# Part of a norm and a weight split moved from the start of the query, key and value projection into the last group of the feed-forward part before it

## The reference, cut to what matters

```python
def _layernorm(x, axis=-1, eps=1e-05):
    m = jnp.mean(x, axis=axis, keepdims=True)
    v = jnp.var(x, axis=axis, keepdims=True)
    return (x - m) / jnp.sqrt(v + eps)

x = x + 0.5 * ffn(_layernorm(x))         # gate and up 512 -> 4096, gelu(gate) * up, down 4096 -> 512
x = x + attention(_layernorm(x))         # 16 heads of 32, causal, 2048 tokens, one batch
x = x + 0.5 * ffn(_layernorm(x))         # the same weights as the first
```

## Time and profile before

| | us |
|---|---|
| median of 3 runs (lowest, highest) | 3058.48 (3055.43, 3061.62) |
| the profiled execution, its own time | 3058.05 |
| its span in the trace | 3056.3 |
| PE busy | 2944.6 (96%) |
| DVE, ACT, POOL busy | 1878.1, 1060.1, 758.6 |
| ffn1: its last down matmul begins at | 1107.10 |
| items 0 to 15: first begins, work behind them begins | 1135.97, 1186.70 |

### The profile page before, as it was taken

How to read it: one execution, slowest core, us unless ns; L and a number is a source line. 1 busy time by engine, 2 the same in 40 slices (tenths; PEclk the granted TensorE clock), 3 DMA queues, 4 the chain that set the end, 5 groups by cost and what they waited for, 6 DMA issues and landing times. The chain is left out here.

```text
span 3056.3 us, 38836 instructions
## 1 busy us (share of the span) xinstructions
PE 2944.6 (96%) x13152; PEld 2208.8 (72%) x13152; DVE 1878.1 (61%) x3314; ACT 1060.1 (35%) x1797; POOL 758.6 (25%) x481
## 2 busy tenths in 40 slices
PE   5999999999999989999999999689999999999999
PEld 3788888888888858754454555368888888888887
DVE  7666565566565555566666665876556656556654
ACT  4322222222222222265565665243222222222222
POOL 4322222222222234400000002343222222222221
PEclk8999999999999989999999999799999999999999
DMA  3000000000000016822322331101000000000001
GB/s 96 21 28 22 27 27 21 21 27 24 24 27 21 1 45 130 220 54 52 62 55 52 62 78 64 45 14 33 23 21 27 21 27 27 21 21 27 21 14 55
DMA packets 120234, 126.75 MB, mean 41 GB/s; under 512 B 72728, under 2 KB 72984, under 8 KB 116820
## 3 DMA queue, kind: packets, MB, share of 16 engines
q1 hardware_dynamic: 120148, 125.71, 15.8%
HBM read 96.34 MB, written 29.34 MB: 41 GB/s over the span
## 5 line engine op out<-in xcount | busy, mean ns | idle before, releaser
L61 PE MATMUL psum<-ffn_x_high,ffn_w_high 128*128 128x512 f32 x2048 | 803.3, 392 | 18.6 <-DVE ffn_gelu L389 18.6
L62 PE MATMUL psum<-ffn_x_low,ffn_w_high 128*128 128x512 f32 x2048 | 799.2, 390 | 0.0
L63 PE MATMUL psum<-ffn_x_high,ffn_w_low 128*128 128x512 f32 x2048 | 798.9, 390 | 0.0
L526 POOL TENSOR_TENSOR ffn_inner<-ffn_gelu,ffn_inner 128x512 fp32r<-128x512 f32 x256 | 345.9, 1351 | 1156.8 <-ACT ffn_inner L471 1156.8
L379 DVE SCALAR_TENSOR_TENSOR ffn_gelu<-ffn_gelu,psum 128x512 f32<-128x512 f32 x256 | 175.9, 687 | 600.0 <-ACT ffn_gelu L464 599.9
L61 PEld LDWEIGHTS psum<-ffn_x_high,ffn_w_high 128*128 128x128 f32 x2048 | 386.1, 189 | 103.9 <-DVE ffn_gelu L389 21.9
L62 PEld LDWEIGHTS psum<-ffn_x_low,ffn_w_high 128*128 128x128 f32 x2048 | 385.9, 188 | 81.9 <-issue 2.0
L63 PEld LDWEIGHTS psum<-ffn_x_high,ffn_w_low 128*128 128x128 f32 x2048 | 385.8, 188 | 80.7
L61 PE MATMUL psum<-ffn_inner,ffn_w_high 128*128 128x512 f32 x1024 | 398.6, 389 | 0.2
L62 PE MATMUL psum<-ffn_inner,ffn_w_high 128*128 128x512 f32 x1024 | 398.4, 389 | 0.0
L63 PE MATMUL psum<-ffn_inner,ffn_w_low 128*128 128x512 f32 x1024 | 398.4, 389 | 0.0
(11 more groups left out here) (116 smaller groups left out, 3191.1 us busy)
## 6 DMA issues: line engine op xcount, KB each, us to landing
ffn_words<-packed SPq DMA_DIRECT2D x96, 256.0 KB
ffn_word_scales<-scales SPq DMA_DIRECT2D x96, 256.0 KB
qk_parts<-parts SPq DMA_DIRECT2D x32, 512.0 KB, 4.3
queries<-qk_parts SPq DMA_DIRECT2D x48, 256.0 KB, 4.1
keys<-qk_parts SPq DMA_DIRECT2D x48, 256.0 KB, 6.1
x<-x_in SPq DMA_DIRECT2D x4, 1024.0 KB, 14.5
v_parts<-parts SPq DMA_DIRECT2D x16, 256.0 KB, 4.7
values<-v_parts SPq DMA_DIRECT2D x16, 256.0 KB, 8.0
```

What stands on the lines that cost most here:

```text
L61: pe.matmul(out, w_high, x_high, start=first, stop=False, skip_group_check=True)
L62: pe.matmul(out, w_high, x_low, start=False, stop=False, skip_group_check=True)
L63: return pe.matmul(out, w_low, x_high, start=False, stop=last, skip_group_check=True)
L526: pool.tensor_tensor(inner[:, tb % 2, m, 1, :], product[m], f32(inner[:, tb % 2, m, 0, :]), ALU.subtract)\
```

## The change

- In ffn1's last group, POOL does `sum_pairs` of tb 0 for the projection's norm between its two tiles of tb 3, once all gate and up products are done and x of tb 0 is final. PE does `mean` 0 before `down(3)`, into bank 0. DVE does `centre` 0 between `add_down` of tb 2 and of tb 3.
- SP issues the load of `wv` when all gate and up products are done. Behind their last tile ACT makes `wv_high` and squares block 0, and POOL makes `wv_low`. All these buffers lie over ffn1's `x_high` and `x_low`, which are read no more then.
- `project_in` begins with `sum_square_pairs` 0 and `variance` 0. The constants (matrix of 1/512, eps, and the buffer `std`) exist once for the program, and are set once.
- In `project_in` PE's list becomes: variance 0, mean 1, mean 2, items 0 and 1, variance 1, items 2 and 3, mean 3, items 4 and 5, variance 2, items 6 to 9, variance 3, items 10 to 15. DVE's and ACT's lists are rearranged with it; `scale` is cut in two, `invert` (the reciprocal) and `scale` (the multiplications), so that an addition of a value item can stand between them.

```diff
@@ class Norm
-        act.activation(self.std[:], self.var_bank[tb % 2], ACT.Sqrt, bias=self.eps[:]).then_inc(self.std_ready, 1)
-
-    def scale(self, dve, tb):
+        act.activation(self.std[:], self.var_bank[tb], ACT.Sqrt, bias=self.eps[:]).then_inc(self.std_ready, 1)
+
+    def invert(self, dve, tb):
         dve.wait_ge(self.std_ready, tb + 1)
         dve.reciprocal(self.std[:], self.std[:]).then_inc(self.rstd_ready, 1)
+
+    def scale(self, dve, tb):
         dve.wait_ge(self.rstd_ready, tb + 1)
@@ class QkvAhead (new)
+        self.norm = Norm(nc, ctx, "qkv", x, None, None, [centred[:, i, :, :] for i in range(2)], squares, pairs[:],
+                         constants.std, constants.averager, constants.eps,
+                         [bank[0], bank[4], bank[5], bank[4]], 2 * bank[6:8], None)
...
+    def high(self, act):
+        act.wait_ge(self.wv_loaded, 16)
+        act.activation(self.wv_high[:], self.wv[:], ACT.Copy).then_inc(self.wv_high_ready, 1)
+
+    def low(self, pool):
+        pool.wait_ge(self.wv_high_ready, 1)
+        pool.tensor_tensor(self.wv_low[:], self.wv[:], f32(self.wv_high[:]), ALU.subtract)\
+            .then_inc(self.wv_low_ready, 1)
@@ ffn, SP
+            if ahead is not None:
+                sp.wait_ge(gate_up_ready, 2 * NTB * NGROUP)
+                sp.dma_start(ahead.wv[:], ahead.w_v).then_inc(ahead.wv_loaded, 16)
@@ ffn, PE, group
+                    elif ahead is not None:
+                        pe.wait_ge(product_ready, 2 * NTB * NGROUP - 1)
+                        ahead.norm.mean(pe, 0)
                     down(gg, s, tb)
@@ ffn, DVE, group
+                    if tb == NTB - 1 and last_group and ahead is not None:
+                        ahead.norm.centre(dve, 0)
                     add_down(gg, s, tb)
@@ ffn, ACT, behind the last group
+            if ahead is not None:
+                ahead.high(act)
+                ahead.norm.square(act, 0)
@@ ffn, POOL, group
+                    if tb == NTB - 2 and last_group and ahead is not None:
+                        gelu_tiles(gg, s, tb + 1, [0])
+                        pool.wait_ge(gate_up_ready, 2 * NTB * NGROUP)
+                        pool.wait_ge(down_free, KT * NTB * (NGROUP - 1) + 2 * KT)
+                        ahead.norm.sum_pairs(pool, 0)
+                        gelu_tiles(gg, s, tb + 1, [1])
...
+            if ahead is not None:
+                ahead.low(pool)
@@ project_in, PE
-            n.mean(pe, 0)
+            n.variance(pe, 0)
             n.mean(pe, 1)
-            n.variance(pe, 0)
             n.mean(pe, 2)
+            pe.wait_ge(ahead.wv_low_ready, 1)
+            value_items(range(0, 2))
             n.variance(pe, 1)
-            pe.wait_ge(wv_low_ready, 1)
-            value_items(range(0, 2))
+            value_items(range(2, 4))
             n.mean(pe, 3)
-            value_items(range(2, 4))
+            value_items(range(4, 6))
             n.variance(pe, 2)
-            value_items(range(4, 8))
+            value_items(range(6, 10))
             n.variance(pe, 3)
-            value_items(range(8, TT))
+            value_items(range(10, TT))
```

More of the change, by code:

```diff
@@ L114, in mean @@
         for k in range(2):
-            last = pe.matmul(self.mean_bank[tb % 2], self.averager[:], self.pairs[:, k, :],
+            last = pe.matmul(self.mean_bank[tb], self.averager[:], self.pairs[:, k, :],
                              start=(k == 0), stop=(k == 1))
@@ L144, in variance @@
         for k in range(2):
-            last = pe.matmul(self.var_bank[tb % 2], self.averager[:], self.squares[:, k, :],
+            last = pe.matmul(self.var_bank[tb], self.averager[:], self.squares[:, k, :],
                              start=(k == 0), stop=(k == 1))
@@ L222, in ffn @@
         n = Norm(nc, ctx, tag, x, x_high, x_low, [centred0[:, :, :], centred1[:, :, :]],
-                 squares[:, :, :], pairs[:, :, :], std, averager, eps,
-                 down_bank[0:2], down_bank[2:4], x_loaded)
+                 squares[:, :, :], pairs[:, :, :], constants.std, constants.averager, constants.eps,
+                 2 * down_bank[0:2], 2 * down_bank[2:4], x_loaded)
         words_loaded = [sem(f"words_loaded{p}") for p in range(NPIECE)]
@@ L314, in group @@
                         gate_up(gg + s, 1 - s, 0)
+                    elif ahead is not None:
+                        pe.wait_ge(product_ready, 2 * NTB * NGROUP - 1)
+                        ahead.norm.mean(pe, 0)
                     down(gg, s, tb)
+            if x_in is not None:
+                pe.wait_ge(constants.ready, 2)
             n.mean(pe, 0)
@@ L407, in group @@
                         unpack(gg + s, 1 - s, tb)
+                    if tb == NTB - 1 and last_group and ahead is not None:
+                        ahead.norm.centre(dve, 0)
                     add_down(gg, s, tb)
-            dve.memset(averager[:], 1.0 / D).then_inc(n.constants_ready, 1)
-            dve.memset(eps[:], EPS).then_inc(n.constants_ready, 1)
+            if x_in is not None:
+                dve.memset(constants.averager[:], 1.0 / D).then_inc(constants.ready, 1)
+                dve.memset(constants.eps[:], EPS).then_inc(constants.ready, 1)
             n.sum_pairs(dve, 0)
@@ L480, in group @@
                         weight_high(gg + s, 1 - s, tb)
-            act.wait_ge(n.constants_ready, 2)
+            if x_in is not None:
+                act.wait_ge(constants.ready, 2)
             weight_high(0, 0, GATE)
@@ L521, in weight_low, with gelu_tiles @@
                                    f32(w_high[s][:, :, piece, :]), ALU.subtract).then_inc(w_low_ready, 1)
-            def gelu_tiles(gg, s, tb):
-                for m in range(2):
+            def gelu_tiles(gg, s, tb, tiles=range(2)):
+                for m in tiles:
                     pool.wait_ge(inner_high_ready, 16 * gg + (8 * s + 2 * tb + m + 1))
@@ L800, in head_items_after, with project_in @@
     return ITEMS_BEFORE[len(ITEMS_BEFORE) * i // (steps + LEFT_TO_LAST):end]
-def project_in(nc, x, bank, w_v, b_v, w_qk, b_qk, qk_parts, v_parts, heads):
+def project_in(nc, x, bank, ahead, b_v, w_qk, b_qk, qk_parts, v_parts, heads):
     with ExitStack() as ctx:
@@ L828, in project_in @@
         parts = sb("parts", [P, ITEM_BANKS, 2, TB], F32R)
-        n = Norm(nc, ctx, "qkv", x, x_high, x_low, [heads.norm_centred[:, tb, :, :] for tb in range(2)],
-                 squares, heads.norm_pairs[:], std, averager, eps, bank[4:6], bank[6:8], None)
-        wv_loaded = sem("wv_loaded")
+        n = ahead.norm
+        n.x_high, n.x_low = x_high, x_low
         bias_loaded = sem("bias_loaded")
         wt_loaded = sem("wt_loaded")
-        wv_high_ready = sem("wv_high_ready")
-        wv_low_ready = sem("wv_low_ready")
         wt_high_ready = sem("wt_high_ready")
@@ L1533, in build @@
         bank = [psum[:, i, :] for i in range(8)]
-        ffn(nc, "ffn1", x, bank, packed, scales, x_in, None)
-        attend(nc, x, bank, w_v, b_v, w_qk, b_qk, w_out, b_out, qk_parts, v_parts, o_heads, sums, inverses)
-        ffn(nc, "ffn2", x, bank, packed, scales, None, out)
+        constants = NormConstants(nc, ctx)
+        ahead = QkvAhead(nc, ctx, x, bank, constants, w_v)
+        ffn(nc, "ffn1", x, bank, constants, packed, scales, x_in, None, ahead)
+        attend(nc, x, bank, ahead, b_v, w_qk, b_qk, w_out, b_out, qk_parts, v_parts, o_heads, sums, inverses)
+        ffn(nc, "ffn2", x, bank, constants, packed, scales, None, out, None)
 def laid_out(L0_attn_x, L0_attn_w_qkv, L0_attn_b_qkv, L0_attn_w_out, L0_attn_b_out,
```

95 lines of the change are left out of this document (51 added, 44 removed).

## The result

The changed kernel takes 3063.14 us (median of 20 runs, 3061.28 to 3066.13), the kernel before, run beside it, 3057.85 us (20 runs, 3053.5 to 3061.62). The ratio is 1.0018, its 95% interval 1.0012 to 1.0025: +5.3 us. The interval leaves out 1, so the change is a little slower, but by less than the 0.2% that the prediction took as the least that can be told from no change. The profiled execution's own time is 3062.0, its span 3060.2.

What follows compares the result with a forecast made beforehand. PE, bound before by the norm's latency and then its own work, becomes a chain of three latencies: 9.9 us won and given back, +0.6, plus 3.6 of clock, is +4.2 on 3058.05, so 3062.3 us; range 3057 to 3069.

Steps and rivals of the forecast that it cites:

- In the first FFN: End of the first FFN: mean 0 moves `down(3)` back by 1.45 us; `centre` 0 and the pairs cost nothing more.
- Cover of wv: First FFN: the load of wv (4.9 us) and its split (4.51 on POOL) finish in time, priced at nothing.
- The sum of squares (1.23): Start of the projection: DVE's sum for block 0 starts at 1110.05 and takes 1.23 us, so the variance begins at 1111.3.
- Block 0's latency: Projection, variance 0 to last low tile: 13.3 to 15.2 us, low 0 ending at 1125.6, 9.9 earlier than before.
- The latencies of blocks 1 to 3: Projection, each variance to its last low tile: 15.0, 14.4 and 13.3 us for blocks 1, 2 and 3.
- It must stand still: PE at items 4, 8 and 12: stalls waiting for low tiles, 5.1 us for block 2 and 4.0 for block 3.
- I take 1.2 per stall: PE's slow clock in the three stalls: 1.2 us each, 3.6 together, between nothing and about 3.1 per stall.
- the first rival: Every stall is followed by a slow stretch costing 3.1 us instead of 1.2: +10.8, 3068.9 us; chance 0.25.
- The reading of the slow rows: Trace before the change: slow stretches lie behind gaps of 2.6 and 7.8 us, with no row for shorter ones in series.
- 3.4 between each two: PE between two latencies: the last quarter of an item and one whole item, 0.68 + 2.72 = 3.4 us.
- 8.84 at the end: Behind block 3's last low tile: the last quarter of item 12 and items 13 to 15, 0.68 + 8.16, to 1187.3.
- The second rival: Projection: the stalls are hidden and PE stays the bound, about -10 us, 3048; chance 0.06.

Runs made afterwards that it cites:

- pool_wait: The changed kernel with POOL's sum of pairs of block 1 waiting until DVE's sum of squares of block 0 is done; 3059.87 us, ratio 1.0008.
- order_only: The kernel before with only the new order of items, variances and additions, nothing moved into the first FFN; 3069.95 us, ratio 1.0035.
- order_back: The changed kernel with PE's item order of before and DVE's additions moved to fit, the moved part kept; 3055.68 us, ratio 0.9992.
- warm: The changed kernel with two unused fp32 matmuls on PE ahead of items 8 and 12; 3062.58 us, ratio 1.0015.
- item_pad2: The changed kernel with 1760 unused bytes per partition ahead of the projection's own buffers; 3061.93 us, one run.
- combined: The changed kernel with the old item order, POOL's pairs behind DVE's squares, and DVE's sums of squares 2 and 3 earlier; 3048.84 us, ratio 0.9973.

## Why the prediction came out, step by step

The forecast was +4.2 (3062.3); measured is +5.3 by the medians (3063.14). Its mechanism stood; some of its terms did not, and errors of both signs met. Down the chain, predicted and measured:

| step | predicted | measured |
|---|---|---|
| last addition, next block | 1109.67, 1110.05 | 1109.30, 1109.63 |
| variance 0 begins | 1111.3 | 1113.09 |
| low 0 ends | 1125.6 (1124.6 to 1126.5) | 1127.97 |
| low 1 ends | 1144.0 | 1146.20 |
| low 2 ends | 1161.8 | 1164.03 |
| low 3 ends | 1178.5 | 1182.74 |
| work behind the items | 1187.3, with the clock 1190.9 | 1192.01 |

- **In the first FFN: right.** `down(3)` moved back by about 1.3 (the last matmul begins 1108.18 here, 6.98 behind mean 0) against 1.45, and the cover held: mean 0 waited for no pairs (0.23 behind the last down matmul), `centre` 0 took 2.29 and was done at 1105.41, the barrier took 0.33.
- **Cover of wv: right.** The load landed in time for ACT to split from 1100.92 to 1102.83, ahead of its squares at 1105.44, and POOL's `wv_low` ran from 1102.91 to 1107.54, before the barrier.
- **"The sum of squares (1.23)": wrong, by 2.17.** I took the duration from a row in which POOL read nothing beside it, although the same sum took 2.31 us where it ran among POOL's low tiles (at 1160.08 before), a slowdown that the prediction itself counts as 1.0 for block 2. POOL's sum of pairs 1 is released by the same barrier. pool_wait shows the price, alone and with its follow-up on variance 0: 3.1.
- **Block 0's latency: right in size** (14.88, within 13.3 to 15.2), though low 0 came outside its bounds, since the start above was late.
- **The latencies of blocks 1 to 3: right.** 15.0, 14.4 and 13.3 predicted, 14.58, 14.17 and 13.22 measured; the addition of item 2 held block 1's multiplications up by 0.4 (to 1138.07, the reciprocal being done at 1137.61), not 0.7.
- **"It must stand still": right.** From the end of the work ahead to the start of the last quarter, less the 2.1 us that three quarters take, the stalls are 3.5 at item 4, 5.0 at item 8 and 3.9 at item 12, predicted 4 (with mean 3 ahead of it), 5.1 and 4.0. order_only shows them without the head, order_back takes them away.
- **"I take 1.2 per stall", the clock: wrong in size and kind.** Behind items 4 and 12 the next steps ran at full clock (3.66 from low 1 to variance 2, as from low 0 to variance 1); only item 8 was followed by a stretch at 0.50, and took 5.49, 1.8 more than its likes. That is 1.8 instead of 3.6, and never 3.1 three times as the first rival had it. Why item 8 and not its likes isn't settled: the pad of 1760 bytes moved the slow stretch to item 12, the fill of warm to item 9, and order_only has one behind item 4 and one behind item 12. What the rows show is that PE did work in quarters in all three stalls, and that one of three was followed by 1.2 GHz, two of three in order_only. The passage of the Trainium skill on a PE that waits between short bursts, named with the first rival, is about waits in one piece; here the quarters cut each stall into waits of at most 1.7 us. As the first rival applied it, it asked for a slow stretch behind all three, and the trace doesn't agree, beyond that one.
- **The reading of the slow rows: incomplete.** The prediction says that the slow stretches of before lie behind gaps of 2.6 and 7.8, and that the trace has no row for shorter ones in series. It has: mean 1 waited 2.49, and variance 0 behind it only 0.83, took 3.78 and ran at half the clock. That series stood for a dearer stall than the 1.2 taken.

```profile
1115.98 2.60 PE L115 MATMUL psum<-qkv_pairs,qkv_averager 128*128 128x512 f32 x4 [2.49 <-POOL qkv_pairs L104]
```

```profile
1118.00:1120.00 2.00, 1.17 (x2) 0.50 (x2) 1.86 (x2) 1.98 (x3) 1.33 (x1) 0.50 0.98 361
```

- **"3.4 between each two", and 8.84 at the end: too short, by 1.2 in all.** At full clock the link from a last low tile to the next variance took 3.66, and the end 9.27. An item at 2.80 instead of 2.72 is the smaller part, some 0.4: in item_pad2, with items at 2.72, a link still took 3.60. The other 0.8 is PE's restart behind a low tile: the last quarter's first matmul begins 0.05 behind the tile, and the next one 0.35 later (1128.02 and 1128.37) instead of 0.23. The prediction put that at nothing.

The sum: 2.2 for the sum of squares, 1.2 for the links and the end, and 0.6 for block 0's latency more than predicted, against 1.8 less on the clock, 0.7 on the latencies of blocks 1 to 3 and 0.4 in the FFN, gives the 1.1 between 1190.9 and 1192.01. That the total is near is in part luck.

The second rival (stalls hidden, -10) needed "low tiles within 9.3 us". combined got its -9 another way: by leaving four items behind variances 2 and 3, together with the two repairs on DVE and POOL. I had the cause in front of me (before, items 4 to 7 hid block 2's 14.4 us) and didn't ask whether the head with the old order would keep both.

## What to carry to other kernels

When work is moved ahead, what it wins is kept only if enough independent work still stands behind each link of the chain: here a variance with four items behind it (11 us, and 4 us for the variance itself and three quarters of the next item) hid the latency of 14, one with two did not, and 12 us won became 5 lost. Price a moved instruction beside what will run with it, not from a row where it ran alone: two engines released by one barrier start in the same moment, and if they exclude each other, the order in which they start should be written down. And when a part of a change is found to lose, try the other part by itself before the whole is dropped.

## What the runs showed that I had not expected

- DVE's sum of squares of 1024 fp32 per partition: 1.23 us alone, 3.40 when POOL's sum of pairs (2.34) had begun 0.02 earlier.
- Matmuls of 128x512 in fp32r: a value item takes 2.80 instead of 2.72 us for its 12, depending on where its operands lie in SBUF alone (remainders by 2048 that are 288 or 320 bytes apart: slow; equal: fast). Whether the distance or the stationary operand's own place decides is open.
- Of three nearly equal stalls of 3.5 to 5 us, fed in quarters, one was followed by PE at 1.2 GHz for some 7 us, and which one changed with small edits elsewhere; with the order alone it was two of three.
